# A token mixer with a routed expert: straight code for the batch loop, three turned planes instead of four, new places for small steps

## What is computed

```python
# B, S, D, M, TOPK = 8, 1024, 256, 4, 2     (attention part, per batch of x)
g, v, d = x @ Wg[m] + bg[m], x @ Wv[m] + bv[m], x @ Wd[m] + bd[m]
a = 0.001 + 0.998 * sigmoid(d)
h = linear_scan(sigmoid(g) * tanh(v), a)            # h_t = a_t * h_{t-1} + x_t, along tokens
comb = one_hot(top2(x @ gate_W)) * softmax(top2 values)
attn = sum over m of comb[..., m] * h[m]
# around it
x = x + layernorm(attn(layernorm(x)))
x = x + layernorm(ffn(layernorm(x)))                # ffn: one expert of 8 for a batch, chosen by its mean token
```

## Time and profile before

| | us |
|---|---|
| median of 3 runs | 679.08 |
| lowest, highest | 678.12, 682.12 |
| profiled execution, its time | 678.97 |
| profiled execution, span of the trace | 677.2 |
| TensorE busy in the span | 618.5 (91%) |
| VectorE busy | 587.4 (87%) |
| ScalarE busy | 461.1 (68%) |
| GpSimd busy | 99.7 (15%) |

### The profile page before, as it was taken

How to read it: one execution, slowest core, us unless ns; L and a number is a source line. 1 busy time by engine, 2 the same in 40 slices (tenths; PEclk the granted TensorE clock), 3 DMA queues, 4 the chain that set the end, 5 groups by cost and what they waited for, 6 DMA issues and landing times. The chain is left out here.

```text
span 677.2 us, 10435 instructions
## 1 busy us (share of the span) xinstructions
PE 618.5 (91%) x3314; PEld 318.4 (47%) x3314; DVE 587.4 (87%) x1094; ACT 461.1 (68%) x791; POOL 99.7 (15%) x101
## 2 busy tenths in 40 slices
PE   3989999999999989999998989999998999899673
PEld 2454454445545535445544535445544554444431
DVE  6799599999899987999899987999899988889866
ACT  3728655896579675896579675896669775877404
POOL 2002011302121101302121101202030102112011
PEclk9979999999999999999999999999999999999687
DMA  8651736154712736054621737045631735211003
GB/s 224 153 187 32 156 62 237 26 111 78 253 60 54 141 101 219 1 106 93 233 80 43 144 100 228 0 96 104 209 104 43 130 99 179 44 31 32 0 22 115
DMA packets 74627, 73.27 MB, mean 108 GB/s; under 512 B 36134, under 2 KB 66122, under 8 KB 74570
## 3 DMA queue, kind: packets, MB, share of 16 engines
q1 hardware_dynamic: 69676, 56.30, 28.8%
q0 software_dynamic: 4896, 16.26, 12.9%
HBM read 38.85 MB, written 8.52 MB: 70 GB/s over the span
## 5 line engine op out<-in xcount | busy, mean ns | idle before, releaser
L1375 PE MATMUL ps_main<-xh,w_hi 128*128 128x512 f16 x768 | 292.5, 381 | 6.9 <-issue 5.7
L1375 PE MATMUL ps_main<-xh,w_lo 128*128 128x512 f16 x768 | 292.4, 381 | 0.0
L1375 PE MATMUL ps_main<-xl,w_hi 128*128 128x512 f16 x768 | 292.3, 381 | 0.0
L914 DVE TENSOR_TENSOR_SCAN hid<-decay_s,hid 128x1024 f32<-128x1024 f32 (+1 forms) x64 | 138.2, 2159 | 6.6
L581 ACT ACTIVATE hid<-ps_main,vecs 128x512 f32<-128x512 f32 x128 | 88.9, 695 | 60.5 <-PE ps_main L1375 60.1
L581 ACT ACTIVATE decay_s<-ps_main,vecs 128x512 f32<-128x512 f32 x128 | 88.9, 695 | 59.1 <-PE ps_main L1375 57.9
L1375 PEld LDWEIGHTS ps_main<-xh,w_hi 128*128 128x128 f16 x768 | 76.1, 99 | 94.6 <-issue 7.8
L581 ACT ACTIVATE gate_s<-ps_main,vecs 128x512 f32<-128x512 f32 x128 | 88.6, 692 | 44.8 <-PE ps_main L1375 43.8
L1375 PEld LDWEIGHTS ps_main<-xl,w_hi 128*128 128x128 f16 x768 | 75.4, 98 | 91.6 <-issue 1.7
L1375 PEld LDWEIGHTS ps_main<-xh,w_lo 128*128 128x128 f16 x768 | 75.3, 98 | 85.7 <-issue 1.1
L932 DVE TENSOR_TENSOR hid<-gate_s,hid 128x1024 f32<-128x1024 f32 (+1 forms) x72 | 79.5, 1105 | 6.5 <-ACT hid L581 6.0
(11 more groups left out here) (152 smaller groups left out, 606.9 us busy)
## 6 DMA issues: line engine op xcount, KB each, us to landing
comb_all<-comb_dram SPq DMA_DIRECT2D x32, 512.0 KB, 5.1
hid<-hid POOLq DMA_DIRECT2D x28, 512.0 KB, 4.6
x_in<-in_L_attn_x SPq DMA_DIRECT2D x16, 512.0 KB, 7.5
resid<-in_L_attn_x SPq DMA_DIRECT2D x8, 1024.0 KB, 6.1
out<-resid SPq DMA_DIRECT2D x7, 1024.0 KB, 5.5
expert<-experts SPq DMA_DIRECT2D x8, 192.5 KB, 2.2
hid<-hid POOLq DMA_DIRECT2D x6, 256.0 KB, 3.3
w_stage<-in_L_attn_Wg SPq DMA_DIRECT2D x4, 256.0 KB, 3.9
```

What stands on the lines that cost most here:

```text
L914: dve.tensor_tensor_scan(states(pc), staged(decay_s, pc, pc.c), states(pc), start, ALU.mult, ALU.add).then_inc(scanned, 1)
L1375: ins = pe.matmul(ps_main[:, i % BANKS], w[:, 3 * m + kind, k, half * P:(half + 1) * P], v[:, bt.par, span(c), k], start=(n == 0), stop=(n ...
```

## The change

- The hardware loop of `iterations` becomes a Python loop: the six middle batches are straight code on every engine.
- `TURNED` is (5, 6, 7): plane 4 is added onto plane 6 by a fifth accumulating transfer, which in a middle batch comes after y's root on GpSimd. TensorE turns three planes, in front of bank 5 instead of 4 (in the last batch still in front of bank 3).
- `move_x` waits for the first addition instead of the second; the second addition, instead of the third, waits for both transposing transfers.
- Steps move within the lists of ScalarE, VectorE and TensorE, mostly in the first batch. In a middle batch: `route_logits` ahead of `low_u`; `weights_of` ahead of plane 6; `finish` and `copy_weights` ahead of plane 7's multiplication (`finish` first); `shares` at bank 43; `turn_weights` in front of bank 45; `router_sigmoids` at 23, `high_rows_x` at 27 and 28, `high_h` at 33.

```diff
-    TURNED = (4, 5, 6, 7)
+    TURNED = (5, 6, 7)
...
-            with eng.Fori(0, B // 2 - 1) as j:
-                for r in (1, 2):
-                    run(turn(j, r), turn(j, r + 1), turn(j, r - 1))
+            for n in range(1, B - 1):
+                run(turn(n // 2, n % 2), turn((n + 1) // 2, (n + 1) % 2), turn((n - 1) // 2, (n - 1) % 2))
...
             def move_x(nx):
                 for a, split, moved in ((0, x_split_hi, xh_moved), (1, x_split_lo, xl_moved)):
-                    sp.wait_ge(plane_added[1], 16 * nx.n)
+                    sp.wait_ge(plane_added[0], 16 * nx.n)
...
             def add_plane(bt, p, c=None):
-                if p == 2 and not bt.cut:
+                if p == 1 and not bt.cut:
                     pool.wait_ge(xh_moved, 16 * bt.n + 16)
...
             def run(bt, nx, pv):          # GpSimd
...
                 power("y", y_root_in, y_root, pv)
+                add_plane(bt, 4)
...
             def run_first(bt, nx):        # ScalarE
                     if i == 0:
                         high_matrix(0, GATE)
                         high_matrix(0, DECAY)
+                        high_matrix(0, VALUE)
                         high_x(bt, 0)
-                        high_matrix(0, VALUE)
+                    if i == 1:
+                        high_gate_weights()
                         mixer_high(1)
                         high_x(bt, 1)
-                    if i == 3:
-                        high_gate_weights()
+                    if i == 4:
+                        mixer_high(2)
                     if i == 6:
-                        mixer_high(2)
-                    if i == 7:
+                        mixer_high(3)
+                    if i == 9:
                         shares(bt)
-                        mixer_high(3)
-                    if i == 21:
+                    if i == 25:
                         normalise_x(nx, tiles(0))
-                    if i == 25:
+                    if i == 26:
                         normalise_x(nx, tiles(1))
-                    if i == 26:
+                    if i == 28:
                         high_rows_x(nx, 0)
...
             x_moments(first, 0)           # VectorE, start
+            scale_x(first, 0)
+            normalise("x", x_in, x_scaled, x_normed, first, 0)
             low_matrix(0, GATE)
-            scale_x(first, 0)
             low_matrix(0, DECAY)
-            normalise("x", x_in, x_scaled, x_normed, first, 0)
+            low_matrix(0, VALUE)
             x_moments(first, 1)
+            copy_vecs()
             low_x(first, 0)
-            copy_vecs()
-            low_matrix(0, VALUE)
...
                 mixer_low(1)              # VectorE, run_first
+                prepare_router(prep)
+                mixer_low(2)
+                rank_mixers(bt)
                 set_ones()
-                rank_mixers(bt)
                 weights_of(bt)
-                mixer_low(2)
-                mixer_low(3)
                 copy_weights(bt, True)
-                prepare_up_biases(prep)
-                prepare_router(prep)
                 prepare_down(prep, 0)
...
+                prepare_up_biases(prep)
+                prepare_hidden_biases(prep)
+                mixer_low(3)
                 x_moments(nx)
...
+                low_rows_x(nx)
                 prepare_up(prep)
-                low_rows_x(nx)
-                rank_mixers(nx)
+                prepare_down(prep, 1)
                 multiply(bt, pcs[4])
                 scan(bt, pcs[4])
                 weigh(bt, pcs[4])
+                rank_mixers(nx)
...
             def run(bt, nx, pv):          # VectorE
...
+                route_logits(pv)
                 low_u(pv)
-                route_logits(pv)
...
                 scale_y(pv)
+                weights_of(nx)
                 multiply(bt, pcs[6])
                 scan(bt, pcs[6])
                 weigh(bt, pcs[6])
-                weights_of(nx)
+                finish(pv)
                 copy_weights(nx, False)
                 multiply(bt, pcs[7])
                 scan(bt, pcs[7])
                 weigh(bt, pcs[7])
-                finish(pv)
...
             def run_first(bt, nx):        # TensorE
-                    if i == 5:
+                    if i == 3:
                         first_gates(bt)
-                    if i == 8:
+                    if i == 11:
                         turn_weights(bt)
                     if i == 15:
                         hidden_bias()
-                    if i == 38:
+                    if i == 40:
                         pe.wait_ge(experts_ready, 6)
                         gates(nx)
...
             def run(bt, nx, pv):          # TensorE
-                    if i == 4:
-                        turn_planes(pv, (4, 5, 6, 7))
+                    if i == 5:
+                        turn_planes(pv, (5, 6, 7))
...
+                    if i == 45:
+                        turn_weights(nx)
                     product(bt, i, bank, False)
-                turn_weights(nx)
```

More of the change, by code:

```diff
@@ L193, in mixer_kernel @@
         weighed = sem("weighed")
-        plane_added = [sem(f"plane_added{p}") for p in range(4)]
+        plane_added = [sem(f"plane_added{p}") for p in range(5)]
         add_go = sem("add_go")
@@ L230, in mixer_kernel, with iterations @@
         MIX_LINKS, ROUTE_LINKS, STAT_LINKS, OUT_LINKS = 8, 6, 3, 1
-        def iterations(eng, run_first, run, last):
+        def iterations(run_first, run, last):
             def turn(j, r):
@@ L441, in last @@
                 sp.wait_ge(out_stored, 16 * (B + 2 * C) + 1)
-            iterations(sp, run_first, run, last)
+            iterations(run_first, run, last)
         @block.gpsimd
@@ L517, in last @@
                 add_plane(bt, 3, 0)
+                add_plane(bt, 4, 0)
                 power("y", y_root_in, y_root, pv)
@@ L526, in last @@
                 power("y", y_root_in, y_root, bt, 1)
-            iterations(pool, run_first, run, last)
+            iterations(run_first, run, last)
         @block.scalar
@@ L697, in run_first @@
                         high_rows_x(nx, 1)
-                    if i == 46:
+                    if i == 41:
                         shares(nx)
@@ L712, in run @@
                         normalise_x(nx, tiles(0))
-                    if i == 24:
                         router_sigmoids(pv)
@@ L717, in run @@
                         high_rows_x(nx, 0)
+                    if i == 28:
                         high_rows_x(nx, 1)
-                    if i == 28:
                         hidden_part(pv, 0)
@@ L724, in run @@
                         high_h(pv, 0)
-                    if i == 34:
+                    if i == 33:
                         high_h(pv, 1)
                     if i == 43:
+                        shares(nx)
                         act.wait_ge(xh_moved, 16 * nx.n)
@@ L732, in run @@
                     if i == 44:
-                        shares(nx)
                         scale_rows(pv, (2, 3), normed)
@@ L782, in last @@
                 scale_late_rows(bt, 1)
-            iterations(act, run_first, run, last)
+            iterations(run_first, run, last)
         @block.vector
@@ L1154, in run_first @@
                 scale_x(nx)
-                prepare_down(prep, 1)
                 multiply(bt, pcs[2])
@@ L1158, in run_first @@
                 weigh(bt, pcs[2])
-                prepare_hidden_biases(prep)
                 multiply(bt, pcs[3])
@@ L1177, in run_first @@
                 scan(bt, pcs[7])
+                copy_weights(nx, False)
                 weigh(bt, pcs[7])
-                copy_weights(nx, False)
             def run(bt, nx, pv):
@@ L1314, in last @@
                 finish_late(bt, 1)
-            iterations(dve, run_first, run, last)
+            iterations(run_first, run, last)
         @block.tensor
@@ L1385, in turn_plane @@
                 pe.wait_ge(weighed, PLANES * pv.n + PLANES * (c or 0) + p + 1)
-                if p < (4 if c else 6):
+                if p < (4 if c else 7):
                     pe.wait_ge(plane_added[p - KT], 16 * (pv.n + (c or 0)) + 16)
@@ L1567, in last @@
                 up(bt, 1)
-            iterations(pe, run_first, run, last)
+            iterations(run_first, run, last)
 _INS = ["L0_attn_x", "L0_attn_Wg", "L0_attn_bg", "L0_attn_Wv", "L0_attn_bv", "L0_attn_Wd", "L0_attn_bd",
```

## The result

| | before | after |
|---|---|---|
| median, us | 678.60 | 662.82 |
| lowest to highest, us | 676.49 to 682.12 | 661.38 to 665.95 |
| ratio after to before, 95% interval | | 0.9744 [0.9696, 0.9792] |
| profiled execution, its time | 678.97 | 662.28 |
| profiled execution, span | 677.2 | 660.2 |

The account below looks back on a forecast made before the run. TensorE's own list was taken as the limit, with VectorE some 6 us behind. Middle batches 13.6, first batch 2.7 and last batch -0.4 made 15.9 us: 678.97 - 15.9 = 663.1 us, range 658.5 to 669.5.

Parts of the forecast that it names:

- The sum: Whole kernel: middle batches 13.6, first batch 2.7, last batch -0.4, together 15.9 us gained.
- A: Whole kernel: the gains come as summed, 663.1 us, within 660 to 665; chance 0.57.
- The loop: Middle batches: straight code removes two taken jumps of TensorE, 3.1 and 3.2 us, together 6.3 us.
- Three planes: Middle batches: one plane fewer saves TensorE 0.9 us each, of which VectorE's later chain takes 0.2 at u's turn.
- B: Middle batches: VectorE's chain behind plane 7 also decides u's turn, batches stay at 75.1, kernel 669.1 us; chance 0.18.
- Transfers and additions: GpSimd and SP queues: moving x's transposing transfers and the additions costs zero and gains zero.
- `route_logits` first: Middle batches: ahead of `low_u`, it brings the expert's transfer 2.4 us earlier and removes `down`'s wait, 0.3 us.
- The first batch: First batch: 2.1 for the router's constants' wait, 1.7 for half clock, less 0.2 and 0.9: 2.7 us gained.
- D: First batch gains nothing if the half clock lasts as long and the later start is not absorbed: 665.8 us; chance 0.12.
- The last batch: Last batch: TensorE loses 0.9 us waiting for planes, VectorE's chain starts about 0.4 later: -0.4 us.
- E: Plane 6's turn: the fifth addition lands late and holds TensorE, kernel slower, 690.7 us at 12 us landing; chance 0.05.

Follow-up runs that it names:

- the small matmuls in four groups: Changed kernel with u normalised in halves, `turn_u` at bank 23, `down` at 29, and first batch's 32 one-column matmuls spread over banks 15 to 18: 659.09 us.
- the router's constants alone: Kernel before, with VectorE running `prepare_router` ahead of `prepare_up_biases` as the only edit: 681.29 us (one run, before 680.2).

## Why the prediction was right, step by step

**The sum** (15.9, measured 17.0): the time lies where A put it, but the three stretches are off by +1.6, -1.3 and +0.8 us, so that the sum is so close owes something to luck.

**The loop** (6.3): right in size by the run with the loop alone (6.7), though the jumps are 5.8 of it and the rest is `down`'s wait, which the prediction put down to `route_logits`. What the prediction had not seen is that the pause does not belong to TensorE: with the other lists it sits on VectorE.

**Three planes** (0.7 net a batch): right, 0.75. The steps behind it held within 0.3 us: plane 7 at 7.4, the statistics at 9.3, t's shift at 28.3, the addition's landing 4.6 us and its cover 2.5 (2.8 forecast). TensorE's longer wait at u's turn took back 0.1 instead of 0.2.

**B** falls as a whole (74.2, not 75.1) and holds in small: VectorE's idle time of 6 us lies elsewhere, so ahead of u's turn it has no slack, and its pauses of 0.46 and 0.31 us pass on to TensorE. That is 0.36 + 0.36 = 0.7 of the 1.3 us by which the six batches fell short. Most of the rest is the cut of the batches of before: from first product to first product they take 75.2, 78.1 and 78.2, so a jump is worth 2.9 to 3.0, not 3.1 and 3.2 (0.4 for the two). An ordinary batch gained 0.99 of the 1.0 forecast, by parts that were a little off: 0.1 more at `down` and 0.1 less lost at u's turn, against a new wait of 0.2 for ScalarE at bank 33 that the prediction had not listed.

**Transfers and additions** at nothing: right in the changed kernel, though the prediction looked at the middle batches only. In the first batch TensorE would wait if the gates stood at bank 38 and the transfers behind the second addition; the gates' place (bank 40) or the moved transfers each prevent it.

**`route_logits` first** (0.3): `down`'s wait is gone (0.4 in an ordinary batch), and it is gone without the straight loop too: everything but the loop has ordinary batches of 74.2, with a wait of 1.29 us at u's turn (1.3 forecast). But the loop alone, with `low_u` first, takes the same wait away, and the changed kernel with four planes has the same ordinary batch, 74.97: on top of the loop, what the move saves ahead of `down`, 0.2 us, comes back as waits for ScalarE at banks 31 to 33. The two edits overlap, so their gains do not add; the forecast counted this wait once, and its 1.0 came out. Only the two batches in which VectorE pauses gain by the moves as well (75.3 and 75.2 with the loop alone, 74.97 with four planes). The prediction also priced the move as if it stood alone. With `low_u` first, the earlier `router_sigmoids` cost some 0.9 us more in each batch.

**The first batch** (2.7, measured 4.3): the terms are 2.1 for the wait (right), -0.3 at bank 11 (-0.2), -0.9 at bank 29 (-0.9), and the clock. That is the step that was mis-sized: "a third" of the half clock's 5.1 us, 1.7, where the stretch went from 10.2 to 3.4 us, 3.4 us of work at full speed. Sum: 2.1 + 3.4 - 0.3 - 0.9 = 4.3. Over the runs: three profiles with the wait had 10.2 us each; ten without it, with the piece undivided, had 0 (one), 3.4 (five) or 6.8 (four), so 4.4 us in the mean, and the removal is worth 2.9 us on average. D falls.

**The last batch** (-0.4, measured 0.4): its timeline of TensorE against the earlier trace rows:

```profile
540.35 1.06 PE L1391 MATMUL ps_aux<-ident,hid 128*128 128x128 f32 x8 [0.33 <-DMA hid<-hid]
542.55 1.09 PE L1391 MATMUL ps_aux<-ident,hid 128*128 128x128 f32 x8 [1.14 <-DVE hid L928]
562.67 1.97 PE L1328 MATMUL ps_aux<-ident,normed 128*128 128x128 f32 x16 [2.19 <-ACT normed L642]
```

VectorE's timeline there, of the kernel before and then of the changed one:

```profile
559.91 2.74 DVE L808 BATCH_NORM_STATS2 stats_a<-ps_aux 128x6 f32<-128x256 f32 x8
...
572.27 0.17 DVE L815 SCALAR_TENSOR_TENSOR moments_t<-moments_t 128x8 f32<-128x8 f32 x1 [0.47 <-DVE moments_t L814]
```
```profile
543.68 2.75 DVE L810 BATCH_NORM_STATS2 stats_a<-ps_aux 128x6 f32<-128x256 f32 x8 [1.19 <-PE ps_aux L1391]
...
555.74 0.17 DVE L817 SCALAR_TENSOR_TENSOR moments_t<-moments_t 128x8 f32<-128x8 f32 x1
```

The waits for planes 6 and 7 are there, and VectorE's chain starts 0.34 us later (8.58 instead of 8.24 us into the batch), as forecast. But the kernel before has one of VectorE's pauses in this batch, 0.47 us between two steps of t's moments, where the changed kernel stops for 0.1. So t's shift is there at 23.4 us in both kernels, u's turn comes at 27.6 in both, and TensorE's wait ahead of it is shorter by the 1.0 us that it lost on the planes. So the delay was priced rightly and a pause that the prediction did not have cancelled it, which is luck; whether it would have reached the end of the batch, no run shows. The 0.4 gained lies in the tail, where the clock's stretches differ from run to run; the lengths of the last batch in the runs above go from 125.1 to 127.1.

**E**: the fifth addition has 2.5 us of cover in an ordinary batch (2.8 forecast). Behind the first batch it is 0.3 us in the changed kernel (it lands at 96.1, TensorE wants it at 96.4), and it is gone with the old first lists (1.83 us of wait) and with the small matmuls in four groups (0.31).

## What to carry to other kernels

When a step is moved, price it together with the steps that the same change moves behind it: undone one by one, the loop, the first lists and `route_logits` cost 7 to 8 us each and the plane 3, together more than the 17 us that all of it brought. The slack that counts is that ahead of the step where the bound engine waits, not the idle time of an engine in the whole batch. And a wait that is removed is worth nothing until the next one on the same engine is named: the router's constants alone gained 3.6 us at bank 17 and had lost them by bank 38. Two edits that take away the same wait, here the straight loop and `route_logits` first, give it once.

## What the runs showed of the hardware

- A taken jump of the same loop cost 3.5 us inside TensorE's branch in one kernel, and 0.2 us there with 5.0 us of pause behind VectorE's branch of 0.06 us in another. Each of these pauses has a transfer of the instruction queues in it (16 KB and 8 KB); TensorE's short jumps have none.
- In straight code VectorE stopped for 0.46 and 0.31 us between dependent steps in the second and the sixth middle batch, at the same two steps in all ten kernels of straight code; where u's turn hangs on VectorE these two batches are 0.3 to 0.4 us longer. Behind each pause an 8 KB instruction transfer starts within 0.6 to 3.7 us, of 21 to 23 in a whole span; that the two belong together is likely, not shown.
- The half clock behind the small matmuls of the first batch lasted 0, 3.4 or 6.8 us with the same lists of that batch, so single times of such kernels can differ by up to 3.4 us for that alone (half of 6.8).
